# Fused adaptive-norm block: row-norm roots, gates, weight rounding and low halves moved between engines, with new issue orders

## The reference

```python
mod = (_silu(c) @ wmod).reshape(8, 6, 1, 128)           # sa, ca, ga, sb, cb, gb per batch
ga = (2 * (ga >= 0) - 1) * max(abs(ga), 0.25)           # gb likewise
h = layernorm(x) * (1 + ca) + sa                        # x is 8 x 1024 x 128
for i in range(6):                                      # DEPTH layers
    xn = layernorm(h) * ln1_w[i] + ln1_b[i]
    q, k, v = xn @ wq[i], xn @ wk[i], xn @ wv[i]        # 8 heads of 16
    q, k = softmax(q, over 16 channels), softmax(k, over 1024 rows)
    h = (q @ (k^T v)) @ wo[i] + bo[i] + h
    xn = layernorm(h) * ln2_w[i] + ln2_b[i]
    h = leaky_relu(xn @ w1[i], 0.01) @ w2[i] + h        # hidden width 512
x = x + ga * h
h = layernorm(x) * (1 + cb) + sb
x = x + gb * fp4_ffn(h)          # gate, up (352 wide), silu, product, down; every operand is
                                 # rounded to fp4 in blocks of 16, with a scale per block
```

## Time and profile before

| | |
|---|---|
| median of 3 runs | 1198.16 us (1198.06 to 1198.7) |
| span of the profiled execution | 1196.8 us |
| busy TensorE / VectorE | 1129.7 us (94%) / 1074.1 us (90%) |
| busy ScalarE / GpSimd | 1035.2 us (86%) / 1090.7 us (91%) |

### The profile page before, as it was taken

How to read it: one execution, slowest core, us unless ns; L and a number is a source line. 1 busy time by engine, 2 the same in 40 slices (tenths; PEclk the granted TensorE clock), 3 DMA queues, 4 the chain that set the end, 5 groups by cost and what they waited for, 6 DMA issues and landing times.

```text
span 1196.8 us, 28581 instructions
## 1 busy us (share of the span) xinstructions
PE 1129.7 (94%) x9722; PEld 864.8 (72%) x9722; DVE 1074.1 (90%) x2885; ACT 1035.2 (86%) x1776; POOL 1090.7 (91%) x920
## 2 busy tenths in 40 slices
PE   7787999999999999999999999999999888999996
PEld 5574687787777777777778778777777755565664
DVE  7889889999999999999999999999987479999973
ACT  5687999999999999999999999999998795767753
POOL 4888999999999999999999999999999888999762
PEclk8799999999999999999999999999999999999998
DMA  8121778768778777687777776866767420110000
GB/s 308 36 71 53 214 213 217 188 209 219 179 205 217 194 216 189 193 221 177 219 212 182 224 202 190 220 194 194 214 188 217 107 61 21 44 37 36 19 19 36
DMA packets 213857, 190.13 MB, mean 159 GB/s; under 512 B 113392, under 2 KB 192080, under 8 KB 213712
## 3 DMA queue, kind: packets, MB, share of 16 engines
q1 hardware_dynamic: 213712, 188.31, 56.3%
HBM read 87.06 MB, written 76.02 MB: 136 GB/s over the span
## 4 chain that ended last, share of the span: by engine, by line
POOL 34%; PE 27%; issue 22%; DVE 10%; ACT 3%; DMA 2%; SPq 2%; DVEq 0%; POOLq 0%; ACTq 0%
POOL hidden L1787 15%; POOL rows_split L1779 6%; POOL arena L1760 4%; POOL arena L1793 3%; PE pair_mlp L576 2%; PE pair_mlp L556 2%; PE ring_pair L615 2%; PE ring_pair L616 2%; PE ring_pair L617 2%; PE pair L567 2%; PE pair L599 2%; DVE ring_pair L1371 2%; DVE arena L1508 2%; PE pair_mlp L674 1%; DVE arena L1389 1%
## 5 line engine op out<-in xcount | busy, mean ns | idle before, releaser
L1787 POOL TENSOR_TENSOR hidden<-hidden 128x2048 f16<-128x2048 f32 x92 | 376.1, 4088 | 0.0
L883 ACT ACTIVATE hidden<-ring_pair,hidden_bias 128x512 f32<-128x512 f32 x384 | 245.6, 686 | 27.9 <-PE ring_pair L617 27.5
L892 ACT ACTIVATE hidden<-hidden 128x2048 f16<-128x2048 f32 x96 | 183.4, 1911 | 17.8 <-PE mlp L633 15.6
L1100 DVE BATCH_NORM_STATS2 bn<-x_all 128x6 f32<-128x128 f32 x896 | 184.2, 278 | 3.2 <-POOL x_all L1739 1.9
L1713 POOL TENSOR_TENSOR rstd<-ve,minus_half 128x8 f32<-128x8 f32 x104 | 170.5, 1640 | 0.0
L852 ACT ACTIVATE arena<-x_all,nmr,rstd 128x128 f32<-128x128 f32 x384 | 157.9, 495 | 0.0
L615 PE MATMUL ring_pair<-arena,halves 128*128 128x512 f16 x384 | 146.1, 381 | 4.5 <-DMA arena<-rows_split 2.8
L616 PE MATMUL ring_pair<-arena,halves 128*128 128x512 f16 x384 | 146.0, 380 | 0.0
L617 PE MATMUL ring_pair<-arena,halves 128*128 128x512 f16 x384 | 145.9, 380 | 0.0
L631 PE MATMUL mlp<-halves,hidden 128*128 128x128 f16 x768 | 135.9, 219 | 1.4 <-POOL hidden L1787 1.4
L633 PE MATMUL pair_mlp<-halves,hidden 128*128 128x128 f16 x768 | 136.5, 220 | 0.0
(11 more groups left out here) (206 smaller groups left out, 3145.1 us busy)
## 6 DMA issues: line engine op xcount, KB each, us to landing
n_away<-all_blocks SPq DMA_DIRECT2D x47, 512.0 KB, 3.3
norm_raw<-n_away SPq DMA_DIRECT2D x188, 128.0 KB, 3.0
k_away<-all_blocks SPq DMA_DIRECT2D x45, 512.0 KB, 2.8
q_away<-all_blocks SPq DMA_DIRECT2D x45, 512.0 KB, 3.3
arena<-k_away SPq DMA_DIRECT2D x180, 128.0 KB, 3.6
arena<-q_away SPq DMA_DIRECT2D x180, 128.0 KB, 3.6
x_all<-in_L_attn_x SPq DMA_DIRECT2D x8, 512.0 KB, 5.4
x_in<-in_L_attn_x SPq DMA_DIRECT2D x8, 512.0 KB, 4.0
```

The lines of the kernel that those rows point to most:

```text
L883: act.activation(hidden_t[:, c * W + h * HALF:c * W + (h + 1) * HALF], ring[n % 2], ACT.Prelu, bias=hidden_bias[:, b:b + 1], scale=HIDDEN_ ...
L892: act.activation(half_rows(hidden_hi, h), half_rows(hidden_t, h), ACT.Copy).then_inc(hidden_hi_ready, 1)
L1100: last = nc.vector.bn_stats(bn[:, 6 * t:6 * t + 6], src(t))
L1787: pool.tensor_tensor(half_rows(hidden_lo, h), half_rows(hidden_t, h), half_rows(hidden_hi, h), ALU.subtract).then_inc(hidden_lo_ready, 1)
```

## The change

It touches the roots, the gates, two preparations and all orders.

- **Roots.** The roots of an item's first norm and of the second norm of the item four before it (`LAG`) become one job on 16 columns. ACT makes a guess, exp(-0.5 ln(variance + eps)) (`root_guess`, two activations); POOL makes one Newton step and the offset in seven small operations (`root_open` to `root_offset`). The powers of `root1` and `root2` go; those of `front_root` and `x_root` stay. An activation table set with both functions is loaded by name at the start. The factor `ROW_SIZE` moves into the root, and out of `ln_cols`.
- **Gates.** A matmul makes the raw gate rows on 8 partitions, DVE computes the gates there in a few operations, and a matmul with `batch_rows` spreads each row over 128 partitions. `prepare_gates` goes.
- **fp4 weights.** Steps 5, 6 and 11 to 16 of `round_weights` run on POOL, the others stay on DVE.
- **Low halves of the MLP weights.** ACT scales the weights in place after writing the high half (12 more activations); POOL subtracts. DVE's step goes.
- **First norm.** Four of eight tiles on POOL instead of three (`POOL_TILES`).
- **Orders.** `keep_warm` and its calls go. Every list `items(v)` is new, rounds count from DVE's statistics on, and all lists run to v = 63.

```diff
+gate_rows, gate_size, gate_sign = k_exp_t[0:B, 0:4 * D], k_exp_t[0:B, 4 * D:6 * D], k_exp_t[0:B, 6 * D:8 * D]
+batch_rows = q_exp[0:B, :]
@@ tensor
+nc.tensor.matmul(ring[1][0:B, :], cond_b.rearrange("p (b k) -> p b k", b=B)[:, :, 0], wmod_s[:, 2 * D:6 * D],
+                 start=True, stop=True).then_inc(mod_in_done, 1)
 pe.wait_ge(mod_in_copied, 2)
+pe.wait_ge(mod_out_steps, GATE_STEPS)
 for b in range(B):
     after(pe, mod_out_copied, b - 1)
-    nc.tensor.matmul(ring[b % 2], tile(cond_b, b), wmod_s[:, 2 * D:6 * D],
+    nc.tensor.matmul(ring[b % 2], batch_rows[:, b * P:(b + 1) * P], gate_rows,
@@ tensor, order of a full round (v between 16 and 50)
+product_q(v - 4); second_mlp(v - 8, 0); second_mlp(v - 8, 1); first_mlp(v - 7, 0); first_mlp(v - 7, 1)
+product_z(v - 5); second_mlp(v - 8, 2); context(v - 5); first_mlp(v - 7, 2); first_mlp(v - 7, 3)
+second_mlp(v - 8, 3); first_mlp(v - 7, 4); first_mlp(v - 7, 5); context_out(v - 5); second_mlp(v - 8, 4)
+first_mlp(v - 7, 6); first_mlp(v - 7, 7); second_mlp(v - 8, 5); second_mlp(v - 8, 6); attend(v - 5)
+second_mlp(v - 8, 7); product_k(v - 3)
@@ scalar
+def root_guess(v):
+    after(act, mv1_ready, min(v + 1, ITEMS))
+    after(act, mv2_ready, min(v - LAG + 1, ITEMS))
+    ...
+    act.activation(root_log[:, :], mv[:, :, 1], ACT.Ln, bias=eps_cols[:, 0:1]).then_inc(root_log_ready, 1)
+    act.wait_ge(root_log_ready, v + 1)
+    after(act, root_steps, rooted(v - 1, ROOTED))
+    act.activation(root_y[:, :], root_log[:, :], ACT.Exp, scale=-0.5).then_inc(root_y_ready, 1)
@@ scalar, prepare_weights
+    act.activation((w1_hi, w2_hi)[n][:, l * HID:(l + 1) * HID], w, ACT.Copy, scale=downs[:, c:c + 1])
+    act.activation(w, w, ACT.Copy, scale=downs[:, c:c + 1]).then_inc(weights_hi_ready, 1)
@@ vector, before the statistics of batch 0
+dve.wait_ge(mod_in_done, 3)
+... (seven operations on 8 partitions)
@@ vector, items
+if v == 0: front_stats(1)
+if v == 0: spread_bias()
+if on(v): bn1_rows(v)
+if on(v): moments1(v)
+if v == 0: front_stats(2)
@@ tensor, items
+if v == 2: output_bias_rows()
+if v == 0: hidden_bias_cols()
+if v == 1: turned_bias_rows()
+if v == 1: turn_first_n(0)
@@ gpsimd, items
+if v == 0: front_root(1)
+if v == 0: front_root(2)
+if v == 0: front_rows(1)
+if rooting(v - 3): root_open(v - 3)
+if rooting(v - 3): root_square(v - 3)
+if rooting(v - 3): root_scale(v - 3)
+if rooting(v - 3): root_newton(v - 3)
+if rooting(v - 3): root_done(v - 3)
+if v == 3: front_root(3)
+if rooting(v - 3): root_offset(v - 3)
+if on(v - 3): normalise1(v - 3)
@@ gpsimd, prepare_weights
+    pool.tensor_tensor(lo[:, l * HID:(l + 1) * HID], stage[n][:, l * HID:(l + 1) * HID],
+                       hi[:, l * HID:(l + 1) * HID], ALU.subtract).then_inc(weights_ready, 1)
```

More of the change, by code:

```diff
@@ L272, in adaln_block, with rooting, rooted @@
         block = ctx.enter_context(nc.Block())
+        LAG = 4
         def on(i):
             return 0 <= i < ITEMS
+        def rooting(v):
+            return 0 <= v < ITEMS + LAG
+        OPENED, SQUARED, SCALED, STEPPED, ROOTED, SHIFTED = range(1, 7)
+        ROOT_STEPS = SHIFTED
+        def rooted(v, step=ROOT_STEPS):
+            return ROOT_STEPS * v + step if v >= 0 else 0
         @block.sync
@@ L514, in _ @@
             mlp0_bank = mlp[0]
-            filler = identity[:, :].bitcast(F16)
-            def keep_warm(bank, count, semaphore=None, value=0):
-                if semaphore is not None:
-                    pe.wait_ge(semaphore, value)
-                for n in range(count):
-                    nc.tensor.matmul(bank[:, 0:2 * P], filler[:, 0:P], filler, start=True, stop=True)
             def turn_first_n(i):
@@ L793, in _ @@
+                if v == 1: turn_first_n(0)
+                if v == 59: product_gate(1, 1)
+                if v == 61: product_gate(2, 0)
+                if v == 54: turn_rows(0)
+                if v == 5: turn_first_k(1)
+                if v == 60: turn_rows(2)
+                if v == 60: product_up(1, 2)
+                if on(v - 3): product_k(v - 3)
+            for v in range(ITEMS + 16):
                 items(v)
@@ L1071, in items @@
-                if v == 50: weights_turned()
-            for v in range(ITEMS + 5):
+                if v == 5: front_hat(3)
+                if v == 56: x_square(0)
+                if v == 57: rows_turned(0)
+                if rooting(v - 4): root_guess(v - 4)
+                if v == 9: copy_q(2)
+                if v == 7: front_hat(5)
+                if v == 62: gate(0, 2)
+                if v == 6: front_hat(4)
+                if on(v - 6): exp_k(v - 6)
+                if v == 7: prepare_weights(0, range(0, 3))
@@ new lines, in items @@
+                if v == 6: copy_k(0)
+                if v == 56: x_epsilon(2)
+                if on(v - 8): second_norm_high(v - 8)
+                if v == 60: x_square(1)
+                if v == 55: x_ties(0)
+                if v == 7: prepare_weights(0, range(3, DEPTH))
+                if v == 61: gate(0, 1)
+                if on(v - 9): copy_hidden(v - 9, 4)
+                if v == 7: prepare_weights(1, range(0, 3))
+                if on(v - 9): copy_hidden(v - 9, 5)
+                if v == 52: x_epsilon(0)
@@ new lines, in items @@
+                if v == 62: x_ties(2)
+                if v == 60: x_hat(2)
+                if on(v - 4): normalise1(v - 4)
+                if on(v - 9): copy_hidden(v - 9, 7)
+                if v == 63: gate(1, 0)
+                if v == 7: copy_k(1)
+                if v == 7: front_hat(6)
+                if v == 55: x_epsilon(1)
+                if v == 8: copy_k(2)
+                if on(v - 9): hidden_high(v - 9, 1)
+                if v == 8: prepare_weights(1, range(3, DEPTH))
+                if v == 58: gate(0, 0)
@@ L1074, in _ @@
+                if v == 54: weights_turned()
+            for v in range(ITEMS + 16):
                 items(v)
@@ L1662, in items @@
-                if v == 53: hidden_tile(2, 0)
-            for v in range(ITEMS + 7):
+                if v == 57: hidden_scale(0)
+                if v == 0: front_stats(3)
+                if v == 53: hidden_low(47, 0)
+            for v in range(ITEMS + 16):
                 items(v)
@@ L1917, in _ @@
+                if v == 6: front_rows(5)
+            for v in range(ITEMS + 16):
                 items(v)
```

681 lines of the change are left out of this document (318 added, 363 removed).

## The result

The changed kernel takes 1219.49 us (median of 4 runs, 1216.97 to 1222.92) where the kernel before takes 1198.11 on the same chip: ratio 1.0174 [1.0147, 1.0200]. The forecast was 1204.0 with a range of 1190 to 1215: the sign was right, the size was not, and the range did not hold the time. The profiled execution has a span of 1215.9 us and belongs to the run of 1217.89.

What follows compares the result with a forecast made beforehand. The middle was taken as bound by TensorE's own work, front and end as other regimes. To the profiled 1196.8 it added -5.2 + 8 + 3 + 0 = +5.8, and 1.4 for the runs' median: 1204.0, range 1190 to 1215.

Steps and rivals of the forecast that it cites:

- Step 1: Roots, middle items: GpSimd saves 2.5 us an item, items come 18.28 apart instead of 18.41, -5.2 us.
- the sum: Added durations and waits along engine queues; over all steps -5.2 + 8 + 3 + 0 = +5.8 us.
- The tight cover at the context product: Middle items: 0.785 us of matmul cover against a 0.72 us path over VectorE, leaving 0.07 us.
- rival (c): Middle: tight waits at context and key products are missed, each item takes 18.59, time 1217; chance 0.12.
- Rival (d): ScalarE: activation tables loaded at each guess, two more loads an item, about 1290 us; chance 0.03.
- Step 2: Front up to item 5: item 0 at 55.7, item 5 at 149.5 instead of 141.87; +8 us, bounds 0 and +14.
- The clock had its own term: Front, fillers removed: key products after longer pauses run at lower clock while ScalarE is busy; 0.4 us.
- Step 3: Rest of the middle: VectorE's gate steps vanish, eight rounding steps go to GpSimd; only cover, worth nothing.
- Step 4: From item 47's key product to the end, 281.9 us before: VectorE idles more at first units; +3 us, bounds -6 and +12.

Runs made afterwards that it cites:

- experiment 4: Changed kernel with the gates' spreading matmuls contracting over 128 rows, 120 of them zero, instead of 8: 1211.96 us, 1.0100.
- experiments 1 and 2: 1: kernel before without its 172 filler matmuls, 1197.75 us. 2: changed kernel with 18 fillers ahead of the gates' spreading, 1217.28 us; with 158 more, 1216.18.
- experiment 9: Changed kernel, 128-row spreading: first rounds and end reordered, 1.0063; item 46's low halves on GpSimd, 1.0145. Changed kernel, end reordered: 1.0287, output wrong.
- experiments 4, 5, 6 and 9: Of these, 5 is the changed kernel with its front reordered, 1211.7 us, 1.0109; with 128-row gate spreading as well, 1208.39 us, 1.0069.
- experiment 6: Changed kernel with its first rounds reordered on every engine, 1217.7 us, 1.0138; another such order with 128-row gate spreading, 1206.97 us, 1.0060.

## Why the prediction was wrong, point by point

**Step 1, the roots and the middle: right, the exact figure partly by luck.** 18.28 an item was forecast, 18.27 measured; GpSimd is at 83 of 100 us ("near 85%"), and TensorE's gaps stay small, as the window below shows. But the sum had 18.27 as the least that an item can take. The undisturbed one takes 18.22 now, and slower ones, of up to 18.9, add 2.2 us to the 42; the two errors cancel.

```profile
150.00:250.00 100.00, 99.17 (x963) 78.64 (x961) 88.94 (x259) 96.42 (x157) 82.98 (x82) 1.00 0.73 210
```

The tight cover at the context product held. Answering to the earlier trace rows, 16 z matmuls, VectorE's scaling and the context product:

```profile
185.30 1.95 PE L583 MATMUL pair_mlp<-arena 128*128 128x128 f32 x16
...
187.75 0.44 PE L592 MATMUL pair_mlp<-small,layer_w 128*128 128x128 f32 x2
```

```profile
187.28 0.35 DVE L1262 TENSOR_SCALAR small<-pair_mlp,ln_cols 128x128 f32<-128x128 f32 x1 [0.41 <-PE pair_mlp L583]
```

VectorE stood waiting 0.41 us, as foreseen, and ends 0.12 us ahead of the context product's start. In every item from 8 to 44 that product follows the last z matmul's start by 0.78 us (0.785 forecast), with no gap. So rival (c) falls. Rival (d) falls as well: the 104 activations of Ln and Exp on 16 columns bring no load. There are two in the whole run, as in the earlier trace rows; the trace agrees with the table set that the prediction quoted.

```profile
L796 ACT ACT_TABLE_LOAD x1 | 1.3, 1283 | 0.8 <-PEq L1976 0.8
```

**Step 2, the start: the step that failed.** +8 was forecast, +19.0 came, 7.0 of the 11 us of error by item 0 and 4.4 between items 0 and 5 (the sum's 149.5 against 160.84; the +8 had 0.4 on top). The first sentence that failed is "TensorE makes that bias only after the 48 small matmuls L510 of 9.42 us, which start near 21.4 as before". They start at 26.74. I had counted the gates' time on VectorE for batch 0's statistics but not for TensorE, whose 16 spreading matmuls now wait for the same gates (+1.7 us); and I gave these 16 their old 7.42 us though each now contracts over 8 rows. They take 11.04 (+3.6), at a clock that falls under way, and leave the low clock to L523 (10.40 instead of 9.42, +1.0) and to L504 (2.70 where the sum had 1.4, +1.3). The bias is spread by 40.7 instead of 33.4, and item 0 comes at 62.7 instead of 55.7.

The second is "that puts item 4 at 131 instead of 121.50, and item 5, with a full TensorE round behind it, at 149.5". Item 4 comes here:

```profile
140.23 1.98 PE L563 MATMUL pair_mlp<-arena,layer_w 128*128 128x512 f32 x4 [2.31 <-ACT arena L818]
```

From item 0 to item 4 that is 77.6 us where the sum had 75.3, and from there to item 5 20.6 where it had 18.5; the earlier trace rows have 20.4 for the latter before the change. ScalarE was forecast without a gap from 73 to 131 us. It is busy 52.92 of 58; the 5.1 idle us, nearly all in its two waits ahead of 100 us, for item 0's transposition L544 and for `hidden_bias`, had no term. Whether they make the 4.4 us was not tested. The clock of the spreading does not: items 0 to 5 take 98.2 us in the kernel after and 98.3 in that of experiment 4.

Experiment 4 takes most of the low clock out and lands at item 5 at 151.6, 2.1 us from the 149.5 of the sum. That nearness is luck. The 9.42 us that the sum had for the one-column products were mostly at the low clock already and become 5.42, so item 0 comes at 53.3, 2.4 us ahead of the sum; items 0 to 5 then lose 4.5 against it. The other profile of this front has 154.8.

The clock had its own term, 0.4 us, placed at the key products, and there it was right: keeping the array busy around them changed nothing (experiments 1 and 2). By the rule of the Trainium skill ("TensorE: Matmul & The Clock Gate", Part 1) the same place would have cost 9 us. That size is near the 9.2 us of experiment 4, by coincidence: the place is another, and the rule, which has the clock follow how busy the array has been, does not foresee a fall in a stretch where the profile has it busy 8.00 of 8 us. The trace decides.

**Step 3, cover: right.** VectorE at 88.9 of 100 us in the middle is nowhere last.

**Step 4, the end: mechanism right, term too small.** +3 forecast, +5.9 measured. The last half of item 47 is added 75 us after its key product (74 forecast, 94 before). The first 120 us from k47 on, before and after:

```profile
914.94:1034.94 120.00, 104.88 (x869) 73.89 (x867) 94.51 (x229) 91.52 (x178) 104.70 (x75) 0.99 0.27 70
928.15:1048.15 120.00, 103.14 (x842) 71.92 (x840) 90.63 (x216) 88.91 (x170) 93.62 (x79) 0.96 0.24 65
```

VectorE's idle time in them rose from 25.5 to 29.4 us (25 to 30 forecast), in the rest from 29.1 to 30.4, and its work over both from 227.3 to 228.0: together the 5.9 us. The sum had set 2 us less of idle time in the drain against 5 more at the first units. In the first 60 us it rose by 0.4 instead of falling, in the second 60 by 3.5, and the last 2.0 us, later idle time and work, had no term. The two other orders of the end in experiment 9 did not mend it.

**Sum.** 1204.0 + 7.0 (up to item 0: the gates' wait and the low clock) + 4.0 (items 0 to 5, less the clock's own 0.4) + 2.9 (end) - 0.6 (middle) = 1217.3. That is the profiled span of 1215.9 with the 1.4 that the forecast adds to a span; the median of the runs is 1219.49. Rival (c) named 1217 with a wait in every item; the total came true, its reason did not.

No kernel with the change's parts beats the kernel before. The best is the one with other orders in the first rounds and 128 rows, 1.0060 [1.0040, 1.0080].

## What to carry to other kernels

When a matmul is rewritten to contract over fewer rows, price it and everything behind it on TensorE at the low clock as well, and try padding the contraction with zero rows: here that cost one memset and took 6.0 and 9.2 us off the path in two profiles. When a measured duration goes into a sum, note the clock that it was measured at. When a producer is put ahead of a fan-out, add its time once for every engine that consumes it, not only for the engine that runs it. Shorter roots and a tighter order belong together: an order that leaves little time ahead of the norm needs the short root.

## What the hardware showed that was not expected

- **TensorE's clock falls while the engine has no idle time.** 16 gapless f32 matmuls over 8 rows: 0.43 us from start to start at 2.4 GHz, 0.85 after the fall, in each of the eight kernels run that spread over 8 rows, 1.5 to 5.0 us behind the first; all 16 took 9.44 to 12.52 us. Over 128 rows, with the same columns and types, they stayed 0.43 us apart to the end in each of the nine profiles with that spreading, 7.4 to 7.5 us in all; five of these nine are of the changed kernel (experiments 4, 5, 6 and 9). The 120 added rows hold zeros, so what differs is the number of rows contracted over and not the values in the first 8; other numbers of rows were not tried.
- **The one-column products share this.** The 48 take 5.42 us when all run at full clock and 10.40 at the low one; before, the 9.42 of the earlier trace rows was mostly at the low clock, which fell 1.1 us behind their first, and one filler for every two of them did not hold it. With 128 rows it fell 0.3 to 4.9 us behind their first in four of the five profiles of the changed kernel.
- **A transposing DMA holds SyncE's queue** 1.25 to 2.91 us in the timelines of experiment 6, with plain ones at 0.3 to 0.6; over the whole profile after, the medians are 1.26 and 0.43. A queue order that is harmless while the front is late becomes a wait of 1.9 us when it is early.
